# Graph attention layer on one core: the first stage in another order

## What is computed

```python
h = jnp.maximum(_layernorm(x, axis=-1), 0.0)
h = h @ W.T + b_W
e = (h @ a1)[:, None] + (h @ a2)[None, :] + b_a[0]
e = jnp.where(e > 0, e, 0.2 * e)
scores = jnp.where(adj > 0, e, NEG_INF)
out = x + jax.nn.softmax(scores, axis=1) @ h
```

## Time and profile before

| | |
|---|---|
| median of 3 runs | 201.71 us (201.53 to 201.79) |
| profiled execution, its own time | 202.36 us |
| its span | 200.8 us |
| granted TensorE clock | 1.00 |
| TensorE matmul busy | 194.9 us (97%) |
| VectorE busy | 183.0 us (91%) |
| ScalarE busy | 147.9 us (74%) |
| GpSimd busy | 52.4 us (26%) |
| HBM | 374 GB/s over the span |

### The profile page before, as it was taken

The page is one execution under the profiler, slowest core; times in us unless marked ns, Lnnn a source line. Parts: engine busy times, 40 slices in busy tenths (PEclk is TensorE's granted clock), DMA queues, the critical chain, the costliest instruction groups (busy, mean ns, idle before and its releaser), DMA issues.

```text
span 200.8 us, 7230 instructions
## 1 busy us (share of the span) xinstructions
PE 194.9 (97%) x3183; PEld 189.2 (94%) x3183; DVE 183.0 (91%) x265; ACT 147.9 (74%) x192; POOL 52.4 (26%) x66
## 2 busy tenths in 40 slices
PE   7969999999999999999999999999999999999993
PEld 7648889999999999999999999999999999999993
DVE  4779999999998799897999999999999999999745
ACT  2679879898882777689988888899588888996000
POOL 1002479699995010205000000072000000510000
PEclk9999999999999999999999999999999999999999
DMA  5999999999999999999999999999999999997012
GB/s 181 376 417 418 407 403 423 421 418 415 422 432 408 418 423 419 416 421 418 415 419 423 419 418 421 421 411 421 419 418 418 415 421 416 418 383 226 6 43 66
DMA packets 15968, 75.66 MB, mean 377 GB/s; under 512 B 1600, under 2 KB 5952, under 8 KB 7616
## 3 DMA queue, kind: packets, MB, share of 16 engines
q1 hardware_dynamic: 15792, 75.06, 91.7%
q10 hardware_dynamic: 144, 0.13, 0.3%
HBM read 73.08 MB, written 2.11 MB: 374 GB/s over the span
## 4 chain that ended last, share of the span: by engine, by line
PE 91%; DMA 4%; SPq 1%; DVE 1%; issue 1%; POOL 0%
PE ps L836 29%; PE ps L834 29%; PE ps L840 29%; DMA adj_sb<-in_adj_t 4%; PE ps L808 2%; PE ps L798 2%; SPq L268 1%; SPq L273 1%; PE ps L876 1%; DVE mask L476 0%; POOL bad L788 0%; DVE rden L504 0%; DVE rg L510 0%; DVE bad L519 0%; DVE upper L576 0%
## 5 line engine op out<-in xcount | busy, mean ns | idle before, releaser
L834 PE MATMUL ps<-V,w 128*128 128x129 f16 x1024 | 174.3, 221 | 0.0
L836 PE MATMUL ps<-V,w 128*128 128x129 f16 x1024 | 174.3, 221 | 0.0
L840 PE MATMUL ps<-V,w 128*128 128x129 f16 x1024 | 174.3, 221 | 0.0
L379 ACT ACTIVATE mask<-adj_sb 128x1024 bf16<-128x1024 int32 x126 | 125.5, 1056 | 28.6 <-DMA adj_sb<-in_adj_t 28.6
L459 DVE SCALAR_TENSOR_TENSOR w<-g_row,pairs,mask 128x1024 f32<-128x1024 f32 x96 | 120.5, 1320 | 5.5 <-ACT mask L379 3.6
L834 PEld LDWEIGHTS ps<-V,w 128*128 128x128 f16 x1024 | 100.2, 98 | 1.5 <-ACT H L340 0.7
L836 PEld LDWEIGHTS ps<-V,w 128*128 128x128 f16 x1024 | 100.2, 98 | 1.0 <-issue 1.0
L840 PEld LDWEIGHTS ps<-V,w 128*128 128x128 f16 x1024 | 100.2, 98 | 0.0
L459 DVE SCALAR_TENSOR_TENSOR w<-ps,pairs,mask 128x1024 f32<-128x1024 f32 x31 | 37.4, 1267 | 0.0
L785 POOL TENSOR_TENSOR xT<-xT,x_sb 128x512 f32<-128x512 f32 x6 | 11.5, 1932 | 79.8 <-ACT xT L394 79.8
L739 POOL TENSOR_TENSOR x_sb<-x_sb,b_row 128x512 f32<-128x512 f32 x8 | 10.0, 1301 | 0.0
(11 more groups left out here) (93 smaller groups left out, 63.8 us busy)
## 6 DMA issues: line engine op xcount, KB each, us to landing
adj_sb<-in_adj_t SPq DMA_DIRECT2D x64, 1024.0 KB, 10.3
xT<-in_x_t SPq DMA_DIRECT2D x8, 256.0 KB, 7.5
x_sb<-in_x_p SPq DMA_DIRECT2D x3, 512.0 KB, 10.9
g_row<-g_dram SPq DMA_DIRECT2D x1, 1536.0 KB, 10.3
out<-xT SPq DMA_DIRECT2D x3, 512.0 KB, 9.9
x_sb<-in_x_p SPq DMA_DIRECT2D x2, 256.0 KB, 4.2
out<-xT SPq DMA_DIRECT2D x1, 192.0 KB, 3.4
out<-xT SPq DMA_DIRECT2D x3, 64.0 KB, 1.6
```

What stands on the lines that cost most here:

```text
L379: nc.scalar.activation(mask[:, m % MASKS, r], adj_sb[:, m % HELD, r], ACT.Relu, scale=CONNECTED).then_inc(mask_ready, 1)
L834: nc.tensor.matmul(sums[:, bank, a, :], w16[:, m % SLOTS, col:col + P, 1], V[:, jt, 0, 0:NF], start=(jt == 0 and a == 0), stop=False, skip ...
L836: nc.tensor.matmul(sums[:, bank, a, :], w16[:, m % SLOTS, col:col + P, 1], V[:, jt, 1, 0:NF], start=False, stop=False, skip_group_check=True)
L840: last = nc.tensor.matmul(sums[:, bank, a, :], w16[:, m % SLOTS, col:col + P, 0], V[:, jt, 0, 0:NF], start=False, stop=(jt == NT - 1), ski ...
```

## The change

The lists of four engines are written in another order, and one transfer becomes two.

- SyncE: tile 0 of adj is loaded as two halves of 0.5 MB. The first (side 0, semaphore `tile_loaded`) goes ahead of xt chunk 3 and x's set 2, the second behind them. `early_mask` waits for the first half alone.
- TensorE: `centre_chunk(0)` comes directly behind the products of ones; the first narrow product follows it, the squares come between the two h chunks, the second narrow product behind them. The squares and cc use other PSUM banks.
- ScalarE: `relu_chunk(0)` ahead of the steps on wp, `take_chunk(0)` ahead of the roots.
- VectorE: `statistics(1)` ahead of the norm; scores and the largest t ahead of cc; gg behind `early_mask`; the reciprocal of the ones (`ones_of(0)`) behind `scale_weights(0)`; all of `statistics(2)`, eight instructions, behind `weigh(0, 1)`.

```diff
--- before.py
+++ after.py
@@ -168,6 +168,7 @@
         adj_loaded = [sem(f"adj_loaded{i}") for i in range(HELD)]
         xt_loaded = [sem(f"xt_loaded{i}") for i in range(NCH)]
         x_loaded = [sem(f"x_loaded{i}") for i in range(len(SETS))]
+        tile_loaded = sem("tile_loaded")
         wp_loaded = sem("wp_loaded")
         b_row_loaded = sem("b_row_loaded")
         constants_ready = sem("constants_ready")
@@ -287,9 +288,11 @@
                 load_x(0)
                 load_x(1)
                 load_xt(2)
+
+                sp.dma_start(adj_sb[:, 0, 0:GC], adj_t[0, :, 0:GC]).then_inc(tile_loaded, 16)
+                load_xt(3)
                 load_x(2)
-                load_xt(3)
-                load_adj(0)
+                sp.dma_start(adj_sb[:, 0, GC:2 * GC], adj_t[0, :, GC:2 * GC]).then_inc(adj_loaded[0], 16)
                 load_xt(4)
                 load_adj(1)
                 load_xt(5)
@@ -399,14 +402,14 @@
 
                 act.wait_ge(constants_ready, 1)
                 nc.scalar.activation(warm[:], zero_col[:], ACT.Sqrt)
+                relu_chunk(0)
                 act.wait_ge(wa_done, 1)
                 nc.scalar.activation(wp[:, WA:WA + 2], ps[:, 5, 0:2], ACT.Copy).then_inc(wa_ready, 1)
                 nc.scalar.activation(wsq[:], wp[:, WT0:WT0 + DOUT], ACT.Square,
                                      scale=(1.02 * DIN) ** 0.5).then_inc(squares_ready, 1)
-                relu_chunk(0)
                 relu_chunk(1)
+                take_chunk(0)
                 roots_part()
-                take_chunk(0)
                 take_chunk(1)
                 nc.scalar.activation(warm[:], zero_col[:], ACT.Exp)
                 relu_chunk(2)
@@ -472,7 +475,7 @@
 
                 def early_mask():
 
-                    dve.wait_ge(adj_loaded[0], 16)
+                    dve.wait_ge(tile_loaded, 16)
                     nc.vector.tensor_scalar(mask[:, 0, 0:GC], adj_sb[:, 0, 0:GC], CONNECTED, 0.0, ALU.mult,
                                             ALU.max).then_inc(mask_early, 1)
 
@@ -563,7 +566,12 @@
                     nc.vector.tensor_tensor(st[:, r, :], H[:, r, 0:2],
                                             rstd[:, 1, r].rearrange("p (n a) -> p n a", a=1).to_broadcast([P, n, 2]),
                                             ALU.mult).then_inc(scores_ready, 1)
-
+                    if part > 0:
+                        ones_of(part)
+
+                def ones_of(part):
+
+                    r = slice(*PARTS[part])
                     nc.vector.reciprocal(H[:, r, ONE], rstd[:, 2, r]).then_inc(ones_ready, 1)
 
                 def pack(part):
@@ -614,31 +622,24 @@
                 nc.vector.tensor_scalar(centre[:], ident[:], -1.0 / DIN, None, ALU.add).then_inc(centre_ready, 1)
 
                 statistics(0)
+                statistics(1)
 
                 dve.wait_ge(norm_summed, 1)
-                nc.vector.tensor_reduce(norm[:], ps[:, 4, 0:DOUT], AX_X, ALU.max).then_inc(norm_ready, 1)
-                statistics(1)
+                nc.vector.tensor_reduce(norm[:], ps[:, G_BANK + 1, 0:DOUT], AX_X, ALU.max).then_inc(norm_ready, 1)
+
+                dve.wait_ge(std_ready, 1)
+                nc.vector.reciprocal(rstd[:, 1, 0:GI], rstd[:, 0, 0:GI]).then_inc(std_ready, 1)
+                dve.wait_ge(std_ready, 2)
+                scores(0)
+
+                dve.wait_ge(scores_ready, 1)
+                nc.vector.tensor_reduce(tt[:, 0:1], st[:, 0:GI, T], AX_X, ALU.max).then_inc(t_limits, 1)
 
                 dve.wait_ge(cc_done, 1)
                 dve.wait_ge(wp_loaded, 16)
-                step_(nc.vector.tensor_scalar(cc[:, 1:2], ps[:, 6, 0:1], wp[:, BA:BA + 1], None, ALU.add))
-                step_(nc.vector.tensor_tensor(cc[:, 0:1], cc[:, 1:2], ps[:, 6, 1:2], ALU.add))
+                step_(nc.vector.tensor_scalar(cc[:, 1:2], ps[:, G_BANK, 0:1], wp[:, BA:BA + 1], None, ALU.add))
+                step_(nc.vector.tensor_tensor(cc[:, 0:1], cc[:, 1:2], ps[:, G_BANK, 1:2], ALU.add))
                 nc.vector.tensor_scalar(cc[:, 1:2], cc[:, 0:1], -SLOPE_OUT, SHIFT, ALU.mult, ALU.add).then_inc(cc_ready, 1)
-
-                dve.wait_ge(std_ready, 1)
-                nc.vector.reciprocal(rstd[:, 1, 0:GI], rstd[:, 0, 0:GI]).then_inc(std_ready, 1)
-                dve.wait_ge(root_ready, 1)
-                step_(nc.vector.tensor_scalar(gg[:, 0:1], root[:], 1e-30, None, ALU.max))
-                nc.vector.reciprocal(gg[:, 1:2], gg[:, 0:1]).then_inc(g_ready, 1)
-                dve.wait_ge(g_ready, 1)
-                dve.wait_ge(std_ready, 2)
-                step_(nc.vector.tensor_scalar(rstd[:, 2, 0:GI], rstd[:, 1, 0:GI], gg[:, 1:2], None, ALU.mult))
-                statistics(2, 0, 3)
-                scores(0)
-
-                dve.wait_ge(scores_ready, 1)
-                nc.vector.tensor_reduce(tt[:, 0:1], st[:, 0:GI, T], AX_X, ALU.max).then_inc(t_limits, 1)
-                statistics(2, 3, 5)
                 dve.wait_ge(t_spread, 1)
                 nc.vector.tensor_reduce(tx[:, 0:1], ps[:, G_BANK + 1, 0:P], AX_X, ALU.max).then_inc(t_bounds, 1)
                 dve.wait_ge(t_bounds, 1)
@@ -647,15 +648,22 @@
                 nc.vector.tensor_scalar(tt[:, 4:5], tx[:, 0:1], -SLOPE_OUT, SHIFT, ALU.mult, ALU.add)
                 nc.vector.tensor_scalar(tt[:, 5:6], tx[:, 0:1], -SLOPE, SHIFT, ALU.mult, ALU.add).then_inc(shift_ready, 1)
                 early_mask()
+
+                dve.wait_ge(root_ready, 1)
+                step_(nc.vector.tensor_scalar(gg[:, 0:1], root[:], 1e-30, None, ALU.max))
+                nc.vector.reciprocal(gg[:, 1:2], gg[:, 0:1]).then_inc(g_ready, 1)
+                dve.wait_ge(g_ready, 1)
+                step_(nc.vector.tensor_scalar(rstd[:, 2, 0:GI], rstd[:, 1, 0:GI], gg[:, 1:2], None, ALU.mult))
                 pack(0)
                 scale_weights(0)
+                ones_of(0)
                 products(0)
                 dve.wait_ge(pairs_ready, 1)
                 weigh_first(0)
                 lows(0)
                 weigh_first(1)
                 weigh(0, 1)
-                statistics(2, 5, 8)
+                statistics(2)
                 weigh(1, 0)
                 weigh(1, 1)
                 products(1)
@@ -848,28 +856,30 @@
                 pe.wait_ge(ones_set, 1)
                 for _ in range(WARM):
                     nc.tensor.matmul(ps[:, 7, 0:P], ones[:], ones[:], start=True, stop=True)
+                pe.wait_ge(centre_ready, 1)
+                centre_chunk(0)
 
                 pe.wait_ge(wp_loaded, 16)
                 nc.tensor.matmul(ps[:, 5, 0:2], wp[:, 0:DIN], wp[:, AV:AV + 2], start=True, stop=True).then_inc(wa_done, 1)
-                nc.tensor.matmul(ps[:, 6, 0:2], wp[:, BW:BW + 1].to_broadcast([P, P]), wp[:, AV:AV + 2], start=True,
+                centre_chunk(1)
+
+                pe.wait_ge(wa_ready, 1)
+                h_chunk(0)
+                pe.wait_ge(squares_ready, 1)
+                nc.tensor.matmul(ps[:, G_BANK + 1, 0:DOUT], ones[:], wsq[:], start=True, stop=True).then_inc(norm_summed, 1)
+                h_chunk(1)
+                nc.tensor.matmul(ps[:, G_BANK, 0:2], wp[:, BW:BW + 1].to_broadcast([P, P]), wp[:, AV:AV + 2], start=True,
                                  stop=True).then_inc(cc_done, 1)
-                pe.wait_ge(centre_ready, 1)
-                centre_chunk(0)
-                pe.wait_ge(squares_ready, 1)
-                nc.tensor.matmul(ps[:, 4, 0:DOUT], ones[:], wsq[:], start=True, stop=True).then_inc(norm_summed, 1)
-                centre_chunk(1)
-                h_chunk(0)
+                centre_chunk(2)
 
                 pe.wait_ge(norm_ready, 1)
-                h_chunk(1)
-                centre_chunk(2)
-
                 pe.wait_ge(t_limits, 1)
                 nc.tensor.transpose(ps[:, G_BANK + 1, 0:P], tt[:, 0:1].to_broadcast([P, P]), ident[:]).then_inc(t_spread, 1)
                 centre_chunk(3)
                 h_chunk(2)
 
                 pe.wait_ge(t_bounds, 1)
+                pe.wait_ge(cc_ready, 1)
                 pe.wait_ge(pairs_ready, 1)
                 for k in range(2):
                     for j in range(CT):
```

More of the change, by code:

```diff
@@ L616, in _ @@
                 statistics(0)
+                statistics(1)
                 dve.wait_ge(norm_summed, 1)
-                nc.vector.tensor_reduce(norm[:], ps[:, 4, 0:DOUT], AX_X, ALU.max).then_inc(norm_ready, 1)
-                statistics(1)
-                dve.wait_ge(cc_done, 1)
-                dve.wait_ge(wp_loaded, 16)
-                step_(nc.vector.tensor_scalar(cc[:, 1:2], ps[:, 6, 0:1], wp[:, BA:BA + 1], None, ALU.add))
-                step_(nc.vector.tensor_tensor(cc[:, 0:1], cc[:, 1:2], ps[:, 6, 1:2], ALU.add))
-                nc.vector.tensor_scalar(cc[:, 1:2], cc[:, 0:1], -SLOPE_OUT, SHIFT, ALU.mult, ALU.add).then_inc(cc_ready, 1)
+                nc.vector.tensor_reduce(norm[:], ps[:, G_BANK + 1, 0:DOUT], AX_X, ALU.max).then_inc(norm_ready, 1)
                 dve.wait_ge(std_ready, 1)
```

(12 more changed lines are left out.)

## The result

| | before | after |
|---|---|---|
| median | 201.99 us (201.53 to 202.95, 7 runs) | 203.29 us (203.17 to 203.92, 7 runs) |
| ratio, 95% interval | | 1.0057 (1.0036 to 1.0079) |
| profiled execution (span) | 202.36 us (200.8) | 203.66 us (202.1) |

The kernel became slower where 201.27 us was forecast. The profiled executions differ by 1.30 us, as the medians do, so their traces can be laid beside each other term by term. Two executions further on lie far outside the others (224.70 us of the kernel with the order alone, 1059.61 us of the kernel before) and are left out of the ratios.

A forecast was written before the change was run, and what follows sets the result against it. TensorE was taken as the bound (2.71 us per `whole`, against 2.50 per adj tile). The front gives 0.89, tile 7's weight lets 0.50 through, tile 3's relu 0.44; the smallest holds: 201.27 us, range 201.05 to 201.8.

The forecast's parts named there:

- The split adds to the landing: Loading tile 0 of adj as two halves makes later tiles land 0.09 us later, with bounds of 0.07 and 0.4.
- The prediction's own sign of being wrong: Wrong if the mask waits, tile 3's landing moves over 0.2 us, or TensorE waits for a weight between tiles 4 and 8.
- The relus before it have room: ScalarE's relus ahead of the one behind tile 3's mask (4 and 5) come early enough not to hold TensorE.
- the relu behind tile 3: ScalarE's relu for h chunk 6, queued after tile 3's mask, lets 0.53 - 0.09 = 0.44 us through, the smallest cap.
- The front: First stage, up to the start of `whole(0)`: it would start at 16.00 us instead of 16.89, a gain of 0.89.
- The landing of the first half: First half of tile 0 lands at 9.6 us, 1.5 us before the early mask needs it.
- Rival 3: First half lands late, so the mask waits with more work behind it: up to 1.12 us slower, 202.8; chance 0.06.
- The cap by tile 7's weight: Statistics moved back delay GpSimd's chain and tile 7's weight by 0.06 us, so TensorE may come only 0.50 earlier there.
- 4: Splitting costs a transfer's fixed time: tile 3 lands 1.6 us later, the kernel is 1.07 slower, 202.8; chance 0.05.

## Why the prediction was wrong

**The step that failed** is "The split adds to the landing", put at 0.09 with bounds of 0.07 and 0.4. Tile 2 landed 2.0 later and tile 3 1.7 later in the first trace; by the means of the groups it is 1.7 and 1.5. Both bounds were rates of transfers that were contiguous in memory. I priced the size of the pieces and the number of transfers, and those cost nothing that shows in the rate or at tile 2; the gaps between the pieces, which no row of before had in them, went unpriced. The source of the half, `adj_t[0, :, 0:GC]`, showed them. The prediction's own sign of being wrong, tile 3 moving by more than 0.2 us, came true; but the unchanged kernel moves it by 0.95 from one trace to the next, so that sign could have shown by chance.

**"The relus before it have room"** fell with it. It held for tiles that land as before. At tile 1 (mask at 16.57, 0.73 later than the forecast landing) and at tile 2 the same queue on ScalarE cost TensorE 0.39 and 1.00. The forecast named only the relu behind tile 3.

**The front** gained 0.53 of the forecast 0.89. Centring of chunk 0 started at 4.79, as forecast, but took 1.35 to end instead of 1.11, so the next started at 6.12 for 5.89; the scores came at 9.97 (forecast 9.78), the mask at 11.40 without a wait (11.12), the pack at 12.64 (12.33), V at 13.59 (13.23). 0.23 came in at the centring, where full clock is recorded from 5.44 us, behind the centring's start; the rest, up to 0.36 at V and at `whole(0)`, in small steps. This gain is one of a pair of traces, too: in the second pair `whole(0)` started at 16.65 before and 16.40 after, and with full clock from 4.15 us (the kernel with the relus first) at 15.99, the forecast's 16.00. The landing of tile 0 at 12.71, from which the forecast measured, is the latest of the five traces that load it in that place (12.23 to 12.47 in the others).

**The landing of the first half**, put at 9.6, was 10.29. With a contiguous half it was 9.24, 9.81 and 9.16, so the working was right for such a one. Rival 3, a mask that waits for it, did not occur: 1.1 us of the margin of 1.5 remained.

**The cap by tile 7's weight** was right as a mechanism, and mattered in no trace of the kernel after, as TensorE was late there anyway. Where the tiles came on time it was what took the gain: with the whole tile early, `whole(0)` started at 16.29, 0.60 ahead of before; 0.12 went at h chunk 6, 0.32 at tile 7, and the 0.16 left is the 0.15 by which the profiled run was shorter (202.21).

**Of the rivals**, 4 had the right size and sign (about 1 us at h chunk 6, 202.8) and the wrong mechanism: a fixed cost of a transfer, which the prediction took from the rule on batching in the Trainium skill ("DMA: Bandwidth & Descriptors", Bandwidth). The contiguous halves are two transfers too and lose no rate (349 to 375 GB/s), so that rule is not what acted here. With no rival for a strided read, slower had only 0.11.

## What to carry to other kernels

A cut of a load along its inner dimension changes how memory is read, not only how many bytes come first: lay each part out contiguously, or load the whole earlier, and look at GB/s while the DMA share stays full. An in-order engine that both prepares late data and feeds the critical engine should do the feeding first: two relus put first took back some 0.5% of the 0.7% that a slow queue had cost. And where a gain ahead of a tuned pipeline is priced, follow it to each later cap; here `whole(0)` came up to 0.90 us earlier, and no trace kept more than 0.24 of it at the last matmul. And before one late landing is explained, look at all of its pieces and at a second trace of the unchanged kernel.

## What was not expected of the hardware

- Reading 4 KB out of every 8 KB took the queue to 277 to 305 GB/s over 5 to 10 us, against 349 to 376 for contiguous reads, with a DMA share of 0.96 to 1.01. In the kernel after, the records of single packets have 208 to 304 ns for a 4 KB piece (means of each half microsecond) from 6.5 to 9.5 us, and 159 ns from 10 us on; with the contiguous halves it is 159 to 176 ns from 7 us on. The second half, as strided, is not slow (420 to 423 GB/s from 10 to 20 us). Why only the first is, stays open.
- TensorE came to full clock between 4.13 and 10.13 us, after work from 1.22 us on, in the late ones without a pause of more than 0.23 us. With the old order of TensorE's list it was behind 9 us in three of six traces (`whole(0)` at 18.3 to 18.8), with the new one never behind 7.33 in eight. Whether the order does this, these numbers don't settle, and the clocks of the runs without a profile aren't known.
- The landing of the same tile in the same kernel moved by up to 1.3 us from trace to trace (tile 3: 25.27 and 26.22 before, 27.01 and 28.30 after). A stop at h chunk 6 of some 0.5 us hangs on it. Much of it is the last of a tile's 16 pieces, which came from 0.01 to 1.66 us behind the fifteenth at tiles 2 and 3; what makes one piece lag is open.
- Two steps of VectorE on 16 columns took 1.05 and 0.97 us beside GpSimd, 0.17 and 0.18 without it.
